# Waiting for the Gelu tiles one by one before the logit matmuls

## The reference

```
xn  = layernorm(x)
# branch 1: gated scan over time
g   = sigmoid(xn @ Wp[:, 0:1024] + b);  k = tanh(xn @ Wp[:, 1024:2048] + b)
u   = xn @ Wu + bu
s_t = g*(s_{t-1}*k + u) + (1-g)*s_{t-1};   y1 = s @ Wo + bo
# branch 2: routing of tokens to 64 slots
h      = gelu([xn, slot_mean] @ w1 + b1)          # 512 wide
logits = (h @ w2 + b2) / (|tau| + 0.1)            # 64 wide
alpha  = softmax over the 8 largest logits, zero elsewhere
slots  = alpha^T @ xn  -> GRU-like update, attention among slots, layer norm, wvp
y2     = (alpha @ slot_values) @ wo + bo2
out = x + y1 + y2
```

## Time and profile before

| | us |
|---|---|
| median of 3 runs | 1812.1 (1811.7 to 1814.25) |
| the profiled execution, its own time | 1818.25 |
| its span on the slowest core (core 4) | 1816.7 |
| spans of the other cores | 1792.6 to 1815.3 |
| mean granted clock of TensorE, core 4 | 0.930 of full speed |
| TensorE busy | 1515.6 (83%) |
| VectorE busy | 751.2 (41%) |
| ScalarE busy | 568.8 (31%) |

### The profile page before, as it was taken

The page is one execution under the profiler, slowest core; times in us unless marked ns, Lnnn a source line. Parts: engine busy times, 40 slices in busy tenths (PEclk is TensorE's granted clock), DMA queues, the critical chain, the costliest instruction groups (busy, mean ns, idle before and its releaser), DMA issues.

```text
span 1816.7 us, 21021 instructions; the slowest of 8 cores (1792.6 to 1816.7 us)
## 1 busy us (share of the span) xinstructions
PE 1515.6 (83%) x7221; PEld 667.9 (37%) x7221; DVE 751.2 (41%) x1359; ACT 568.8 (31%) x926; POOL 27.0 (1%) x54
## 2 busy tenths in 40 slices
PE   0089989899898998989989899899734379999998
PEld 0044444444444444444444444444311123333333
DVE  0135456364454645646446464564502112222222
ACT  0242524335253352533525425242101121111120
POOL 0100000000000000000000000000011000000000
PEclk9998999899899999999999999999966679899898
DMA  9542020210202102022020220201199345555555
GB/s 150 130 73 93 1 93 1 93 73 22 93 1 93 65 29 93 1 93 78 16 93 1 93 93 1 93 1 47 53 163 170 69 155 186 185 196 198 185 186 208
DMA packets 42680, 166.52 MB, mean 92 GB/s; under 512 B 4290, under 2 KB 5458, under 8 KB 41682
## 3 DMA queue, kind: packets, MB, share of 16 engines
q1 hardware_dynamic: 36178, 134.29, 20.5%
q0 software_dynamic: 6400, 30.89, 10.3%
HBM read 128.68 MB, written 67.11 MB: 108 GB/s over the span
## 4 chain that ended last, share of the span: by engine, by line
PE 70%; DMA 10%; DVE 9%; issue 4%; DVEq 3%; ACT 2%; ACTq 0%; SPq 0%; POOL 0%; POOLq 0%
PE psA L1041 8%; PE psA L437 6%; PE psA L442 6%; PE psC L449 6%; PE psC L442 6%; PE psB L449 6%; PE psB L437 6%; PE psA L511 4%; PE psA L299 3%; PE psC L1041 3%; PE psB L1041 3%; PE psB L511 3%; DVEq L102 3%; DMA sb_bq_c<-bq_pk 3%; DMA sb_WT<-Wih_pk 2%
## 5 line engine op out<-in xcount | busy, mean ns | idle before, releaser
L19 ACT ACT_TABLE_LOAD x83 | 106.5, 1283 | 392.4 <-PE psA L511 388.6
L481 DVE SCALAR_TENSOR_TENSOR sb_a_sb<-sb_g_sb,sb_s_sb 128x512 f32<-128x512 f32 x128 | 88.7, 693 | 275.7 <-PE psB L449 151.6
L1041 PE MATMUL psA<-sb_wo_sb,sb_z_f 128*128 128x512 bf16 x512 | 140.8, 438 | 20.3 <-ACT sb_z_f L1010 18.6
L493 DVE TENSOR_TENSOR_SCAN sb_ys_bf<-sb_a_sb,sb_ys_bf,sb_b_sb 128x512 bf16<-128x512 f32 x120 | 154.0, 1284 | 9.0
L1056 DVE TENSOR_TENSOR sb_prd<-psA,sb_prd 128x1024 f32<-128x1024 f32 x32 | 39.2, 1225 | 256.6 <-DMA sb_prd<-out 173.7
L437 PE MATMUL psA<-sb_xn_f,sb_Wp_sb 128*128 128x512 bf16 x512 | 125.8, 390 | 0.0
L299 PE MATMUL psA<-sb_Wo_sb,sb_ys_bf 128*128 128x512 bf16 x512 | 118.3, 379 | 5.7 <-DVE sb_x_sl L327 5.7
L442 PE MATMUL psA<-sb_xn_f,sb_Wp_sb 128*128 128x512 bf16 x512 | 121.5, 380 | 0.0
L442 PE MATMUL psC<-sb_xn_f,sb_Wp_sb 128*128 128x512 bf16 x512 | 121.0, 379 | 0.0
L449 PE MATMUL psB<-sb_xn_f,sb_Wu_sb 128*128 128x512 bf16 x512 | 120.9, 379 | 0.0
L449 PE MATMUL psC<-sb_xn_f,sb_Wu_sb 128*128 128x512 bf16 x512 | 120.9, 379 | 0.0
(11 more groups left out here) (224 smaller groups left out, 1883.8 us busy)
## 6 DMA issues: line engine op xcount, KB each, us to landing
sb_x_sl<-x SPq DMA_DIRECT2D x32, 1024.0 KB, 6.9
out<-sb_x_sl SPq DMA_DIRECT2D x32, 1024.0 KB, 4.6
sb_prd<-out SPq DMA_DIRECT2D x16, 2048.0 KB, 11.0
out<-sb_prd SPq DMA_DIRECT2D x32, 1024.0 KB, 4.9
sb_WT<-Wih_pk POOLq DMA_DIRECT2D x12, 512.0 KB, 8.8
sb_whh_pp<-Whh_pk POOLq DMA_DIRECT2D x12, 512.0 KB, 8.5
sb_Wp_sb<-Wp_pk POOLq DMA_DIRECT2D x1, 4096.0 KB, 34.3
sb_Wu_sb<-Wu_pk POOLq DMA_DIRECT2D x1, 2048.0 KB, 36.9
```

The source lines that it names most:

```text
L19: return eng.add_instruction(mybir.InstLoadActFuncSet(name=eng.bass.get_next_instruction_name(), act_func_set_id=idx, ins=[], outs=[]))
L481: P.op("ve", lambda v, pp=pp: v.scalar_tensor_tensor(t.a_sb[:], t.g_sb[:, pp, :], -2.0, t.s2_sb[:, pp, :], ALU.mult, ALU.mult))
L493: P.op("ve", lambda v, j=j, init=init: v.tensor_tensor_scan(t.ys_bf[:, j, :], t.a_sb[:], t.b_sb[:], init, ALU.mult, ALU.add), inc="sve", e ...
L1041: P.op("pe", lambda e, i=i, f=f, k=k, ps=ps, p2=p2: e.matmul(ps[:, f * 512:(f + 1) * 512], t.z_f[:, p2 % 2, k, i * 128:(i + 1) * 128], t.w ...
```

## The change

The wait for the last Gelu (`hf` of block NH - 1) before the logits goes. In its place, ahead of each of the four matmuls of token tile i = 0, stands a wait for the Gelu of the block that this matmul reads. The claim of C0 now stands ahead of these waits. The matmuls and their order stay as they are.

```
-        P.wait("pe", ("hf", ph, NH - 1))
         pe_claim("C0")
         for i in range(TPT):
             for kh in range(NH):
+                if i == 0:
+                    P.wait("pe", ("hf", ph, kh))
                 P.op("pe", lambda e, i=i, kh=kh: e.matmul(
                     t.psC[:, i * 64:(i + 1) * 64],
                     t.h_f[:, kh, i * 128:(i + 1) * 128], t.w2_sb[:, kh, :],
```

## The result

The kernel got slower. Medians over 30 runs each: 1813.8 us before, 1817.5 after; the ratio is 1.0029, with a 95% interval of 1.0019 to 1.0039, so about 5.3 us. The loss is not a fixed step: the changed kernel's times spread from 1813.8 to 1828.7, those of the kernel before from 1809.7 to 1816.0. I had forecast 1810.6 and no change that can be told, and the time lies above my range.

The account below looks back on a forecast made before the run. TensorE, busy 83% of the span, was taken to bound the kernel. Savings of 1.4 + 1.5 = 2.9 us, half given back by the clock, made 1812.1 - 1.45 = 1810.6 us; range 1806.0 to 1815.4.

Parts of the forecast that it names:

- (a): Three of twenty logit matmuls per piece move into the hole before the last Gelu: 1.4 us saved, at most 3.4.
- (b): C0's claim comes before the wait for the last Gelu: 0.10 us saved in each of 15 pieces, 1.5 us.
- (c): Three waits added on TensorE's queue find their Gelu done and cost nothing; without the hole's cover 4.8 us.
- (d): ScalarE evicts the logits earlier, nothing on the path waits for that; no DMA, DVE, POOL or SP instruction is touched.
- (e): Clock dips around the hand-over to the next piece give back half of the 2.9 us saved, leaving -1.45.
- Rival 3: Slower: double dips added at L437 after the logits and L511 before, 3.2 us each; two give 1817.0; chance 0.10.
- rival 2: Denser hole and logits stretch, one double dip fewer on the slowest core: 1807.4; chance 0.22, two other ways included.
- the sign that I had named: The prediction is wrong if the number of double dips on the slowest core changes by two or more.

Follow-up runs that it names:

- fill2_before: The kernel before with 13 unread matmuls per piece among the transposes and three in the hole before the last Gelu's logits: 1791.8 us, ratio 0.9874.
- fill2_after: The changed kernel with 13 unread matmuls per piece among the transposes and three in the hole before the last Gelu's logits: 1788.8 us, ratio 0.9861.
- the seven kernels of the table: Changed kernel plain or with one, two or four added Gelu waits; kernel before with C0's claim moved or one or two added waits: ratios 0.9980 to 1.0034.
- c0_first: The kernel before with only C0's claim put ahead of the wait for the last Gelu: 1810.3 us against 1812.6, ratio 0.9992.

## Why the prediction was wrong, step by step

**(a), (b): right, in mechanism and size.** The moved matmuls run in the hole, and the claim of C0 before the Gelu's wait gives 0.14 in place of 0.24. 1.71 became 1.52, as written. `fill2_before` and `fill2_after` measure the two together at 0.19 us of a piece, 2.7 us in fourteen.

**(c): right.** The early waits cost nothing that shows: they stand in `fill2_after`, and its pieces are shorter by the whole 0.19. A wait that stands behind Gelu 3 does cost 0.106.

**(d): right.** No other engine's work or waits changed.

**(e): the step that failed** is "between all kept (0 given back) and all given back (2.9)". The upper end was wrong: the clock can take back more than the whole saving. The direct 2.7 to 2.9 and the measured loss of 5.3 make some 8 us taken back, where I had put 1.45. My picture was that of a dip that stays in its place while the piece slides earlier under it, which can at most cancel the saving. That this picture is incomplete shows in the pieces of core 3: the number of hand-overs with a dip isn't fixed. In the kernel before, a dip lengthened its piece and the next hand-over had none; with pieces 0.19 shorter the next one can have one as well, and one of the two is longer. A pair then takes 153.3 in place of 150.2.

**Rival 3** had the right sign and half of the place. It added double dips, on the L511 matmuls and on the L437 ones after the logits. Low clock was added on L511 only; the dips after the logits went away, which is what **rival 2** said, and the sign that I had named, a change by two or more double dips on the slowest core, came true (core 4 had three, and core 7, now the slowest, has none from piece 1 on) without the kernel getting faster. Both halves of the clock's answer happened at once, and I had priced them as alternatives. I gave slower 0.08: the seven kernels of the table, all within 0.25 us of the old length of a piece, span 5 per mille, so a saving of 1.6 per mille could not be given a sign from its own size. The rows held the warning, a double dip at 3.2 us against a saving of 2.9 in all, and I used it only for the edge of the range.

**What stays open.** Why 0.10 less per piece is good and 0.195 less is bad is shown only as a fact about this kernel; no experiment set out a rule for which hand-over gets a dip. That all of the 5.3 us is lost in the first stage is inferred: the profiles are of one execution each, and the stages weren't timed one by one over many runs.

The Trainium skill ("TensorE: Matmul & The Clock Gate", section "What's actually happening") has the clock's monitor run free of the kernel. The experiments fit that and don't test it: a wait that does no work changes which pieces run slow. The same section ties the low clock to an idle TensorE. The rows here neither confirm nor refute that: in the stretch ahead of a dip in the kernel before, TensorE's row is busy 2.58 of 4.20 us, 1.44 of it with transposes (L355, L412), and the longest wait is 1.60.
```profile
475.00:479.20 4.20, 2.58 (x25) 1.55 (x23) 2.79 (x7) 0.00 (x0) 0.00 (x0) 1.00 0.66 226
```

## What to carry to other kernels

When the granted clock dips at a recurring place of a loop and one dip costs more than the whole saving that is being judged, the saving's sign is open until the dips are gone: first fill TensorE's idle time there with matmuls that nobody reads, then judge. Here the same edit was worth +5.3 us without fillers and about -2.7 where fillers had removed all dips, and -14.0 where the fillers had left dips that it removed itself. A superfluous wait is a cheap probe: here adding one made the kernel faster, which no cost of the new order can explain.

## What the runs showed of the hardware that I had not expected

A satisfied wait on TensorE's queue costs 0.10 to 0.11 us where it stands behind the one that released the engine (0.24 against 0.14, and the same step in `c0_first`; with one, two and four added, the first logit matmul starts 0.25, 0.36 and 0.57 us after the Gelu's end, against 0.14). Thirteen idle-time matmuls per piece, about 2.8 us of TensorE work, saved 8.6 us alone and 22.6 us with three logit matmuls moved into a hole. And a matmul of 64 columns starts 0.03 us after another, but at the change between 128 rows and the one-row bias matmul it is 0.13 (259.42, 259.54 and 259.67 are three such starts in piece 2 of the changed kernel), and one bias matmul in place of four, with kh outermost, leaves 0.59 us between the last Gelu's end and the first L437 where the changed kernel has 1.52.
